# Attention with relative positions: turned scores built in PSUM, the exponential taken from there, and pairs of fp16 planes on two row tiles

## The reference

```python
Q, K, V = heads(xn @ W.T + b)                      # B=2, H=16 heads, L=2048, dk=16
rel_pos = arange(L)[None, :] - arange(L)[:, None] + 255
rel_k, rel_v = relative_k[rel_pos], relative_v[rel_pos]   # 511 rows; negative indices wrap, large ones clip
scores = einsum('bhld,bhrd->bhlr', Q, K) / sqrt(dk) + einsum('bhld,lrd->bhlr', Q, rel_k)
attn = softmax(scores)
out = einsum('bhlr,bhrd->bhld', attn, V) + einsum('bhlr,lrd->bhld', attn, rel_v)
out = out @ Wo.T + bo
ffn: softmax router, top 2 of 8 experts, silu(g) * u, down projection
```

## Time and profile before

| | us |
|---|---|
| median of 3 runs | 4175.11 (4165.85 to 4184.01) |
| profiled execution | 4160.9 |
| span of its trace | 4159.6 |

### The profile page before, as it was taken

The page is one execution under the profiler, slowest core; times in us unless marked ns, Lnnn a source line. Parts: engine busy times, 40 slices in busy tenths (PEclk is TensorE's granted clock), DMA queues, the critical chain, the costliest instruction groups (busy, mean ns, idle before and its releaser), DMA issues. The chain is left out here.

```text
span 4159.6 us, 173466 instructions
## 1 busy us (share of the span) xinstructions
PE 3599.3 (87%) x60310; PEld 3086.1 (74%) x60310; DVE 3312.0 (80%) x9926; ACT 2952.8 (71%) x4828; POOL 2954.0 (71%) x3233
## 2 busy tenths in 40 slices
PE   7689889898989898988888889898988999699991
PEld 4377777777777777777777777777777788558990
DVE  7598989888988888888898888888888989644443
ACT  3488878787878787878787878787778888325440
POOL 3488878787878787878787878787878887560005
PEclk9799999999999999999999999999999999759995
DMA  7755555555555555555555555555555555461224
GB/s 257 238 180 173 178 165 180 162 170 163 175 164 175 167 174 165 175 169 174 176 175 170 175 168 175 165 173 166 173 165 175 178 173 179 158 205 57 62 65 129
DMA packets 385646, 693.17 MB, mean 167 GB/s; under 512 B 62986, under 2 KB 190739, under 8 KB 383619
## 3 DMA queue, kind: packets, MB, share of 16 engines
q1 hardware_dynamic: 378498, 663.88, 49.9%
q0 software_dynamic: 6144, 16.79, 1.2%
HBM read 336.76 MB, written 343.49 MB: 164 GB/s over the span
## 5 line engine op out<-in xcount | busy, mean ns | idle before, releaser
L819 POOL TENSOR_TENSOR pt_near<-pt_full,pt_near 128x512 f16<-128x512 f32 (+3 forms) x2176 | 2069.5, 969 | 614.2 <-DVE pt_near L1089 598.3
L1057 DVE CUSTOM_DVE_ANT_0 scores<-pb,skewed 128x512 f32<-128x512 f32 (+3 forms) x2592 | 1396.3, 574 | 455.3 <-PE pb L857 222.1
L1013 ACT COPY pt_full<-pb 128x512 f32<-128x512 f32 x2048 | 1156.4, 585 | 543.1 <-PE pb L870 503.3
L870 PE MATMUL pb<-ident,scores 128*128 128x128 f32 x8192 | 1282.7, 280 | 50.0 <-issue 49.4
L1089 DVE CAST pt_near<-pt_full 128x512 f16<-128x512 f32 (+3 forms) x2176 | 1195.9, 592 | 0.3 <-ACT pt_full L1013 0.3
L870 PEld LDWEIGHTS pb<-ident,scores 128*128 128x128 f32 x8192 | 1031.2, 146 | 183.5 <-issue 63.1
L917 PEld LDWEIGHTS pb<-pt_near,table_high 128*128 128x128 f16 x18432 | 924.4, 97 | 254.9 <-issue 119.4
L917 PE MATMUL pb<-pt_near,table_high 128*128 128x64 f16 (+6 forms) x18432 | 993.9, 188 | 134.3 <-POOL pt_far L819 68.9
L1004 ACT ACTIVATE scores<-scores,exp_bias 128x2048 f32<-128x2048 f32 x512 | 1026.9, 2006 | 54.2 <-DVE exp_bias L1071 52.7
L917 PE MATMUL pb<-pt_near,table_low 128*128 128x64 f16 (+6 forms) x9216 | 945.1, 188 | 0.0
L857 PE MATMUL pb<-k_stack,q_stack 96*128 96x512 bf16 x2048 | 800.3, 391 | 45.7 <-DVE part_max L1057 43.3
(11 more groups left out here) (170 smaller groups left out, 3373.9 us busy)
## 6 DMA issues: line engine op xcount, KB each, us to landing
rel_scratch<-rel SPq DMA_DIRECT2D x896, 256.0 KB, 2.3
skewed<-rel_scratch SPq DMA_DIRECT2D x256, 576.0 KB, 4.0
rel_scratch<-rel SPq DMA_DIRECT2D x288, 128.0 KB, 2.1
skewed<-rel_scratch SPq DMA_DIRECT2D x64, 512.0 KB, 4.2
skewed<-rel_scratch SPq DMA_DIRECT2D x64, 448.0 KB, 4.1
planes_scratch<-planes SPq DMA_DIRECT2D x32, 384.0 KB, 2.7
q_stack<-planes_scratch SPq DMA_DIRECT2D x192, 64.0 KB, 3.9
k_stack<-planes_scratch SPq DMA_DIRECT2D x192, 64.0 KB, 4.3
```

Source lines behind the costliest of these rows:

```text
L819: ins = nc.gpsimd.tensor_tensor(pt_piece(c, 1, a, z, near), pt_full[e][:, (a - 4 * g) * P:(z - 4 * g) * P], pt_piece(c, 0, a, z, near), AL ...
L870: ins = nc.tensor.transpose(t_ps[g % 2][:, i * P:(i + 1) * P], scores[u % 2][:, blk * P:(blk + 1) * P], keep["ident"][:, :])
L1013: nc.scalar.copy(pt_full[e][:, :], t_ps[ACT_GROUPS[e] % 2][:, :]).then_inc(s_ea, 1)
L1057: ins = nc.vector.tensor_tensor_reduce(out=scores[k % 2][:, a:z], in0=ps[:, a - bank * CH:z - bank * CH], in1=other, scale=1.0, scalar=-3. ...
```

## The change

- `project`: Q and K are kept as two fp16 planes (high, low) instead of three bf16 planes. K is stored in three kinds: plain, and with the left or the right end row of the relative table added into its bias (so the constant far part of the relative term comes out of the score matmul). That makes eight tiles per chunk (`NFULL`) of two planes, 256 KB each, instead of four of 384 KB. ScalarE writes the high plane straight from PSUM (L420), VectorE the low one (L487), GpSimd nothing.
- Stacks: three plane products of 16 rows (48 rows) instead of six (96), laid out twice: partitions 0 to 47 hold keys 0 to 1023, partitions 64 to 111 keys 1024 to 2047. PE works on them in two row tiles of 64 partitions, alternating.
- The table of relative keys has 768 columns in two halves (the part that wraps around is stored a second time by DMA).
- Scores are computed only to find the maximum (`search_bank`, VectorE): add and maximum in the window, a plain maximum outside; no scores are kept. The maximum, scaled and split in fp16 (`maximum_high`, `maximum_low`), is turned by a matmul together with the queries (`max_rows`, PE) and copied to SBUF as `q_max` (`query_rows`, ScalarE).
- `turned_scores` (PE): for each 128-block the scores minus the maximum are built already turned in PSUM: in the window a transpose of the skewed block (7.5 blocks per unit on average, 120 over the sixteen c), and on top, for all sixteen blocks, a matmul of 50 rows.
- `exponentials` (ScalarE): four instructions of 128 x 512 from PSUM into `pt_full`. The row sums come from a column of ones in V (`VW` = 33 columns instead of 48).
- Casts: three groups on VectorE, the fourth on ScalarE. GpSimd's `low_part` is as before; its preparation of V has 8 stages per head instead of 14.
- PSUM: four banks in rotation instead of three, two for turned scores. Four `skewed` buffers instead of two, lags one shorter. SyncE waits for the store of a step's relative products and issues the skewed read in the same step.
- At the start of `attend` GpSimd fills four blocks of the key stacks with a constant before SyncE may load the stacks.

What each function now does, cut to the core:

```diff
-LAG_SKEW, LAG_S, LAG_E, LAG_T, LAG_PV = 2, 3, 4, 5, 6
+LAG_S, LAG_A, LAG_X, LAG_PV = 2, 3, 4, 5
-    scores = [("scores", k - LAG_S, bank) for bank in range(L // CH)] if k >= LAG_S else []
-    return scores + [("rel", k, n) for n in range(rel_groups(k % NB))]
-BANKS = 3
+    return [("scores", k - LAG_S, 0), ("scores", k - LAG_S, 2), ("rel", k, 0), ("rel", k, 1),
+            ("scores", k - LAG_S, 1), ("scores", k - LAG_S, 3), ("max", k - LAG_A, 0)]
+BANKS = 4
...
+            def turned_scores(it, u, pair):
+                c, b = u % NB, (u // NB) % 2
+                if pair == 0:
+                    pe.wait_ge(s_q, it * STEP + u + 1)
+                steps = (2 * pair, 2 * pair + 1)
...
+                    if 4 * u + e >= 2 and (near[e] or e % 2):
+                        pe.wait_ge(s_exp, it * (4 * STEP) + 4 * u + e - 1)
+                    for blk in near[e]:
+                        nc.tensor.matmul(x_ps[e % 2][:, (blk - 4 * g) * P:(blk - 4 * g + 1) * P],
+                                         skewed[u % 4][:, col:col + P], keep["ident"][:, :], is_transpose=True,
+                                         start=(blk == near[e][0]), stop=False)
...
+                        ins = nc.tensor.matmul(x_ps[e % 2][:, i * P:(i + 1) * P],
+                                               k_stack[b][tile_rows(tile, STACK + 2), kind_of(c, blk), col:col + P],
+                                               q_max[u % 2][tile_rows(tile, STACK + 2), :],
+                                               start=(i == 0 and not near[e]), stop=(i == 3))
...
             def step(it, k):            # ScalarE
+                turning = exists(it, k - LAG_X)
+                if turning:
+                    exponentials(it, k - LAG_X, 0)
+                    exponentials(it, k - LAG_X, 1)
+                if exists(it, k):
+                    for n in range(2):
+                        rel_evac(it, k, n)
+                if turning:
+                    exponentials(it, k - LAG_X, 2)
+                    exponentials(it, k - LAG_X, 3)
+                    high_part(it, k - LAG_X, 3)
+                if exists(it, k - LAG_A):
+                    query_rows(it, k - LAG_A)
...
             def step(it, k):            # VectorE
-                    add_bank(it, a, 2)
-                    add_bank(it, a, 3)
+                    search_bank(it, a, 1)
+                    search_bank(it, a, 3)
                 if turning:
                     high_part(it, t, 2)
-                    high_part(it, t, 3)
                 if adding:
                     raw_maximum(it, a)
...
+                    maximum_high(it, a)
+                    maximum_low(it, a)
...
+            for i in range(2):          # GpSimd, before the first load of the stacks
+                for tile in range(2):
+                    nc.gpsimd.memset(k_stack[i][first:first + ROW_TILE // 2, :, :], MAX_SCALE).then_inc(s_kset, 1)
```

## The result

The kernel after the change took 4265.35 us (4 runs, 4245.5 to 4306.87), the kernel before 4176.48 beside it: ratio 1.0228, 95% interval 1.0147 to 1.0308. It is slower, by 2.3% (the interval leaves 1.5 to 3.1%); predicted were 3770 us and a range of 3590 to 3990. The profiled execution's span is 4269.7 us with a mean granted clock of 0.870, against 4159.6 and 0.942.

The account below looks back on a forecast made before the run. No engine was full: VectorE and PE waited for each other through three rotating banks. With 5.80 us per unit, 4160.9 - 415 + 15 + 10 - 5 = 3766, predicted as 3770 us, range 3590 to 3990.

Parts of the forecast that it names:

- the sum of the loop: Attention loop: 5.45 us plus loop turn and stalls gives 5.80 us per unit instead of 6.61, -415 us over 512 units.
- the turn of the loop (0.22): Hardware loop's turn every 32 units: VectorE idle for 7.03 us, counted as 0.22 us per unit.
- stalls in the ring: Attention loop: 0.13 us per unit added for waits between ScalarE and PE.
- the ring: Attention loop: ScalarE's query-row copy, PE's turned scores and the next exponential wait in turn; 5.45 us per unit taken.
- the old knot opens: Attention loop: with four banks, VectorE and PE no longer wait for each other through the rotating banks each step.
- the second sign of being wrong: Attention loop: the prediction called itself wrong if PE waits on a bank of the rotation.
- The skewed read: Attention loop: read lands some 10.7 us after the step began, hidden because the search wants it at 13.0.
- Taken were 5.0 us: PE's work per attention unit, between 4.78 with row tiles fully overlapping and 5.82 with no overlap.
- The exponential out of PSUM: ScalarE in the attention loop: four per unit, 0.687 us each, within 4.73 us of ScalarE work.
- 5.17 taken: VectorE's work per attention unit: 5.71 less 0.69 for casts plus 0.15 for one more tiny operation.
- Rival 3: Attention loop slower: VectorE casts wait for GpSimd subtractions over the shared port; kernel at 4330 us, chance 0.08.
- Outside the loop: Projection stores +15 us, fills at the start of `attend` +10, one pipeline step fewer -5.

Follow-up runs that it names:

- e9: Kernel before the change, with score and relative products contracting over 32 of the 96 stacked rows; 4667.1 us (one run).
- e7: Changed kernel, with the next head's stacks and values loaded from ScalarE's queue instead of SyncE's; 4193.3 us, ratio 1.0055.
- e13: Changed kernel, with scores, maxima, turned scores and values one step later behind the relative products, nothing else; 4167.9 us, ratio 0.9981.
- e5: Changed kernel, with the row maximum's high part as a VectorE reduction and its low part as a ScalarE activation; 4223.2 us, ratio 1.0123.
- e10: Changed kernel with e2, e5, e7, picked values spread over three steps, and scores through values one step later; 4062.8 us, ratio 0.973.
- e2: Changed kernel, with score and turned-score products on all 64 rows of a row tile instead of 48 and 50; 4245.7 us, ratio 1.0166.
- e17: e10 with the picked values of a half back in one step, as in the changed kernel; 4063.1 us, ratio 0.9732.
- e14: e10 with score and turned-score products back on 48 and 50 rows instead of 64; 4081.1 us, ratio 0.9775.
- e1: Changed kernel, with the maximum's low part taking the high part as per-row scalar, one tensor input; 4250.5 us, ratio 1.0198.

## Why the prediction was wrong, step by step

**The step that failed** is the sum of the loop: "To 5.45 I add the turn of the loop (0.22) and, for stalls in the ring, 0.13". It has no term for the clock. I had read 0.97 in the earlier trace rows and carried it over. By the comparison place by place the term is at most some 380 us, 0.75 us per unit. The other part is the 0.13 for stalls, which was too small: "the old knot opens" did not come true, and with the clock up the step is 6.06 and not 5.80. PE still waits on the banks of the rotation, the second sign of being wrong, 202 us in 2900 in after where before has 160:

```profile
PE pb L885 <- DVE part_max L1102: 106.1, 137, 3.9
PE pb L885 <- DVE part_max L1106: 96.2, 133, 3.5
```

```profile
PE pb L849 <- DVE part_max L1057: 123.4, 170, 1.5
PE pb L857 <- DVE part_max L1057: 36.1, 41, 1.4
```

No run reached 5.80 at the full clock: with all places weighted alike they have 5.9 to 6.4 us, and what holds the best of them there stays open. What brings the clock down:

- *Waits of TensorE.* Falls follow them in every trace (1.4 to 2.4 us idle of the 5 ahead, against 0.4 to 0.6 elsewhere and 0.02 in e9). e7 and e13 take waits of VectorE away and leave TensorE's work as it is; TensorE's waits over 0.8 us go from 188 to 148 and 130 us, the share from 0.221 to 0.187 and 0.170, and the mean clock of the executions from 0.869 to 0.875 up to 0.881 to 0.890 and 0.885 to 0.893. e5 is weaker (0.204, clock 0.877 to 0.883, TensorE's waits no shorter), and which waits count is not shown: e10 has more of them than after at half the share. I expected stalls to be passed around the ring at their own price. The edits add up: e13, e7, e5 and e2 alone give 2.5, 1.7, 1.0 and 0.6% of before's time, 5.9 in sum; all four together (e17) give 5.0.
- *Thinner work.* Rows alone are worth 18 to 20 us in two pairs (e2, e14). That is shown for the clock, less firmly for the time. That the rest of the gap to before (e13's 90 falls at half of before's long waits, behind shorter ones) is thinness too, products on 48 rows two at a time and 33 columns instead of 48 in the values, is only argued: each such product is half the work of the one it replaces. It stays open.

**The skewed read** was the second error, and the one that could have been seen. I had written "some 10.7 us after the step began; the search wants it ... at 13.0", and that I would be wrong if it was what the search waits for. It was: the store lands after 4.1 to 4.4 us instead of 2.3 and the read after 4.6 instead of 4.0.

```profile
skewed<-rel_scratch SPq DMA_DIRECT2D x256, 576.0 KB, 4.6
rel_scratch<-rel SPq DMA_DIRECT2D x416, 319.5 KB, 4.4
rel_scratch<-rel SPq DMA_DIRECT2D x320, 320.0 KB, 4.1
```

```profile
DVE part_max L1106 <- DMA skewed<-rel_scratch: 92.4, 72, 3.6
```

With 5.8 us steps that is 10.7 + 2.0 + 0.6 = 13.3 against 2 x 5.8 + 1.4 = 13.0. I took the landing of the old stores, though the change cuts each block into longer and fewer ones, and I left out the next head's loads on the same in-order queue (e7). Each of the two edits that give the read more time brings a large part of the loss back, 97 us (e13) and 72 (e7).

**The terms of the sum**, by the trace:

- PE's tiles overlap: two products of 512 columns start at 2000.89 and the next pair at 2001.11, 0.22 us for two; the turned scores' eight at 2000.66 take 0.23. Taken were 5.0 us; its four mode changes (3.97 per unit in the trace) cost some 0.1 us each by e9, and steps at c = 10 to 15 take 5.6 to 5.8. By the rule of the Trainium skill that I weighed (TensorEngine Tiling (Array Packing), Key Properties) both halves hold here, the overlap by the 0.22 us for two and the drain by e9's 0.1 us per change.

```profile
2000.66 0.40 PE L927 MATMUL pb<-q_max,k_stack 50*128 50x128 f16 x8
2000.89 0.38 PE L885 MATMUL pb<-k_stack,q_stack 48*128 48x512 f16 x2
2001.11 0.32 PE L871 MATMUL pb<-rk_stack,q_stack 48*128 48x384 f16 x2
```

- The exponential out of PSUM: 0.687, as taken. The ring itself is slack: TensorE waits for the query rows' copy for 4.4 us in the whole stretch.

```profile
PEld pb L919 <- ACT q_max L1061: 4.4, 26, 0.2
```

- VectorE: 5.17 taken. In after it is busy 2524.4 / 2900 x 6.80 = 5.92. The two operations on two elements take 0.29 and 0.86 on average where one of 0.15 was and one more of 0.15 was priced: 0.84 too little per unit, more than the whole difference. L1071 works on one element per row.
- Rival 3 named the right mechanism and the wrong instructions: it charged the casts (mean 0.565, no longer than before), while the operations of two elements wait for a whole subtraction. In time that is e5's 42 us and not 4330 - 3770. By the Trainium skill (SBUF — State Buffer, on the shared port pair) the lock holds for a whole instruction; the traces agree, 1.02 us beside GpSimd's subtractions of 1.15 to 1.19.
- Outside the loop the forecast holds. The first stack load is issued at 171.63 (about 174 said), the first product starts at 181.46 instead of 167.58, the first exponential at 195.5 instead of 179.8: 15.7 us later where 15 + 10 - 5 = 20 were forecast.

```profile
166.19 5.36 POOL L853 MEMSET k_stack<- 32x3072 f16 x2
...
171.63 0.34 SPq L698 DMA_DIRECT2D q_stack<-planes_scratch  x1
...
181.46 0.82 PE L871 MATMUL pb<-rk_stack,q_stack 48*128 48x384 f16 x3 [43.35 <-DMA k_stack<-planes_scratch]
```

An outcome that I gave 0.08 (slower at all) came true by a way that no rival had. The rivals were all ways in which work or waits grow; none let the same work run at another speed.

## What to carry to other kernels

Read the granted clock beside the busy share before and after a change, and give the clock a term of its own: this change won 0.29 us per unit at the full clock (6.35 to 6.06), left TensorE's waits, and lost more than that at the lower level. Do not take the difference of fast and slow intervals for the clock's cost; compare like places. When steps get shorter, work out again by how much every transfer is ahead of its use, with the landing times of the new shapes; a stage set one step later costs one step once and brought 2.5% here. Price a small operation by a row with the same count of elements and the same operands, and look at what GpSimd does beside it.

## What the runs showed of the hardware

- An operation of VectorE on 128 x 2 elements in SBUF takes 0.17 us with GpSimd idle; beside GpSimd it took over 0.3 us in 457 of 507 cases, 1.02 at the median, with one tensor input as with two (L1130 in e1 and after); a reduction on the same elements takes 0.162 us and never more than 0.166, though it starts beside GpSimd 171 times (e5).
- Two products on different row tiles cost the time of one (0.22 us for 2 x 512 columns). A change between tiles and the whole array costs 0.1 us net (e9), and products on 32 rows can so cost more than on 96 (e9, 7.10 us per step against 6.35).
- A GpSimd fill of 32 x 3072 fp16 elements takes 2.68 us, near the 2.87 of 96 x 3328 fp32: by these two the time goes with the columns, 0.87 and 0.86 ns each, and neither with rows nor with bytes.
- After a fall in the loop the lower clock lasted 4.5 us on average in before, 6.4 in after and 28 in e9, where TensorE waits for nothing but its products are thinnest.
- The clock is higher with more rows in the same products: 0.888 to 0.900 on 64 rows of a tile (e2) against 0.869 to 0.875 on 48 and 50 (after), 0.919 to 0.922 (e10) against 0.909 to 0.911 (e14).
